# A fused attention and FFN block on one core: first batches brought forward, last contexts by groups, the first maxima's scores made twice

## The reference

```
xn  = (x - mean) / sqrt(var + 1e-5)                      # over the channels
q, k, v = xn @ w.T * s + b                               # 128x128 each, 16 heads of 8 channels
ctx = softmax(q k.T / sqrt(8)) v                         # by head, 256 x 256 scores
att = ctx @ w_o.T * s_o + b_o
h   = s0 * [xn, -xn] @ (+1 or -1 by k0)                  # 256 -> 512
h   = s1 * (2 relu(h)) @ (+1 or -1 by k1)                # 512 -> 512
ffn = s2 * (2 relu(h)) @ (+1 or -1 by k2)                # 512 -> 128
out = x + att + ffn
```

## Time and profile before

| | us |
|---|---|
| median of three runs (lowest, highest) | 313.89 (313.88, 314.91) |
| profiled execution | 313.65 |
| its span | 311.8 |
| PE busy in the span | 280.5 (90%) |
| DVE, ACT, POOL busy | 245.7, 224.8, 131.9 |
| mean granted clock of TensorE | 0.981 |

### The profile page before, as it was taken

One profiled execution on the slowest core, in us unless ns is written; L12 is line 12 of the kernel. 1 busy time (PEld: TensorE's weight loads), 2 busy tenths in 40 slices (PEclk: granted clock), 3 DMA queues, 4 the chain that ended last, 5 costly groups with the idle time before them and its releaser, 6 DMA issues.

```text
span 311.8 us, 8673 instructions
## 1 busy us (share of the span) xinstructions
PE 280.5 (90%) x3220; PEld 179.1 (57%) x3220; DVE 245.7 (79%) x367; ACT 224.8 (72%) x373; POOL 131.9 (42%) x315
## 2 busy tenths in 40 slices
PE   5387879999999999999999999999999877799993
PEld 5255546666666666656666666666666443355651
DVE  4714975889898989898998989898989787688632
ACT  2425356888788787878797888887887867477880
POOL 5233543526363636354454536273636343111201
PEclk9999977999999999999999999999999999799999
DMA  4231323213231414232322223241314141400000
GB/s 122 68 95 38 90 74 90 78 56 102 70 107 52 129 54 125 58 106 61 99 85 88 96 71 112 58 125 48 111 49 127 38 129 36 128 21 4 21 16 20
DMA packets 27387, 23.84 MB, mean 76 GB/s; under 512 B 4674, under 2 KB 24146, under 8 KB 27346
## 3 DMA queue, kind: packets, MB, share of 16 engines
q1 hardware_dynamic: 27218, 22.89, 24.7%
q10 hardware_dynamic: 128, 0.39, 0.4%
HBM read 15.47 MB, written 7.34 MB: 73 GB/s over the span
## 4 chain that ended last, share of the span: by engine, by line
PE 73%; DVE 17%; issue 3%; ACT 3%; POOL 1%; DMA 1%; ACTq 0%; POOLq 0%; DVEq 0%
PE work L947 19%; DVE neg_max L687 14%; PE max_pair L915 14%; PE work L1002 12%; PE exp_pair L935 6%; PE work L970 5%; PE work L1017 5%; PE work L989 4%; PE work L1026 3%; PE work L976 2%; PE work L963 1%; DVE r_lo L713 1%; ACT probs L522 1%; ACT r_hi L576 1%; DMA xin<-x 1%
## 5 line engine op out<-in xcount | busy, mean ns | idle before, releaser
L687 DVE TENSOR_REDUCE neg_max<-max_pair 128x4 f32<-128x1024 f32 x124 | 151.1, 1219 | 34.7 <-PE max_pair L915 32.1
L522 ACT ACTIVATE probs<-exp_pair 128x1024 f32<-128x1024 f32 x124 | 126.5, 1020 | 33.0 <-PE exp_pair L935 31.5
L947 PE MATMUL work<-probs,v_ext 128*32 128x256 f32 x1024 | 62.9, 387 | 0.7 <-ACT ffn L609 0.7
L1002 PE MATMUL work<-r_hi,w 128*128 128x256 f16 x256 | 62.2, 282 | 1.1 <-DVE r_lo L713 1.1
L1002 PE MATMUL work<-r_lo,w 128*128 128x256 f16 x256 | 61.9, 280 | 0.0
L915 PE MATMUL max_pair<-k_rows,q_rows 48*128 48x256 f16 x496 | 49.0, 276 | 11.3 <-DVE neg_max L687 8.5
L713 DVE SCALAR_TENSOR_TENSOR r_lo<-work,r_hi 128x512 f16<-128x512 f32 x64 | 43.3, 677 | 15.9 <-ACT r_hi L576 15.9
L935 PE MATMUL exp_pair<-q_rows,k_rows 51*128 51x256 bf16 x496 | 48.2, 272 | 0.5 <-ACT probs L522 0.5
L576 ACT ACTIVATE r_hi<-work 128x512 f16<-128x512 f32 x64 | 37.8, 591 | 11.4 <-PE work L1002 7.3
L947 PEld LDWEIGHTS work<-probs,v_ext 128*32 128x32 f32 x1024 | 30.5, 111 | 24.6 <-issue 7.7
L915 PEld LDWEIGHTS max_pair<-k_rows,q_rows 48*128 48x128 bf16 x496 | 14.2, 94 | 44.2 <-DVE neg_max L687 23.0
(11 more groups left out here) (102 smaller groups left out, 385.6 us busy)
## 6 DMA issues: line engine op xcount, KB each, us to landing
q_rows<-q_scratch SPq DMA_DIRECT2D x64, 96.0 KB
k_rows<-k_scratch SPq DMA_DIRECT2D x60, 96.0 KB
q_scratch<-q_part SPq DMA_DIRECT2D x16, 192.0 KB, 2.0
xin<-x SPq DMA_DIRECT2D x16, 128.0 KB, 2.2
k_scratch<-k_part SPq DMA_DIRECT2D x16, 128.0 KB, 1.8
out<-outs SPq DMA_DIRECT2D x16, 128.0 KB, 1.8
q_rows<-max_rows SPq DMA_DIRECT2D x64, 6.0 KB
k_rows<-k_scratch ACTq DMA_DIRECT2D x4, 96.0 KB
```

The lines of the kernel that those rows point to most:

```text
L522: nc.scalar.activation(probs[p // GROUP][:, first:first + 2, :, :].rearrange("p h k q -> p (h k q)"), exp_banks(b, p)[:, :], ACT.Exp, scal ...
L687: nc.vector.tensor_reduce(out=neg_max[:, p // GROUP, :, p % GROUP, :], in_=max_banks(b, p)[:, :].rearrange("p (x q k) -> p x q k", x=2, q=TT),
L947: last = mm(bank[VC * j:VC * (j + 1), g * SEQ:(g + 1) * SEQ], v_ext[b % 2][:, kt, HALF * half + head, :], probs[half][:, head, kt, :], sta ...
L1002: last = mm(bank[:, (m % 2) * SEQ:(m % 2 + 1) * SEQ], w1[:, kk, m * P:(m + 1) * P], part[:, kk, :], start=kk == n == 0, stop=kk == FB - 1 ...
```

## The change

The tables are retimed. Batches 1 to 3 get their input work much earlier, from four buffers instead of two or three. The FFN of batches 0 and 1 comes one slot earlier, that of batches 14 and 15 eight slots later than its place instead of sixteen. At the start the attention weights are loaded from ACT's queue, x of four batches early, the FFN weights with a semaphore each. v_ext is zeroed and k_rows filled with ones by DVE (the first k_rows before the statistics of batch 0, the others in slots -4 and 2), instead of POOL's memsets and the DMAs of ones. DVE scales batch 0's q, POOL forms its xT_lo, SP issues its k rows. The scores for the maxima of batches 0 and 1 are computed twice into the same banks. The last batch's second context half is done by its two groups, and DVE alone normalises the last batch's contexts.

```diff
-PE_AT = {"maxT0": 5, "maxT1": 9, ..., "ctx1": 16, "ctx0": 12, "v": 1, ..., "xT": -13, "l0b": -9}
-ACT_AT = {"q_mid": -7, ..., "max0": 5, "v": 1, ..., "max1": 8, ...}
-POOL_AT = {"q_lo": -6, "k_lo": -8, "split0": 4, "split1": 7, "q_rest": -7, "xT_lo": -11, "norm": -18,
-           "xres": -12, "ctxn": 19, "y": 3}
-SP_AT = {"rows": -3, "max0": 7, "k_store": -5, "q_store": -4, "x": -24, "out": 24, "max1": 11}
+PE_AT = {"maxT1": 9, "o": 22, "maxT0": 5, ..., "ctx1": 16, "v": 2, "ctx0": 12, ..., "ctx2": 16}
+ACT_AT = {"q_mid": -7, "v": 2, ..., "max0": 4, "max1": 9, ...}
+POOL_AT = {"k_lo": -8, "norm": -17, "split1": 7, "xres": -10, "q_rest": -7, "q_lo": -7, "xT_lo": -11,
+           "split0": 3, "y": 3, "ctxn": 20}
+SP_AT = {"out": 24, "max1": 11, "max0": 7, "rows": -2, "q_store": -4, "x": -23, "k_store": -6}
...
-FFN_LATER = {0: -7, 1: -1, BATCH - 2: 16, BATCH - 1: 16}
-INPUT_WORK = ("norm", "xT", "xT_lo")
-INPUT_LATER = {1: -22}
+FFN_LATER = {0: -8, 1: -2, BATCH - 2: 8, BATCH - 1: 8}
+INPUT_WORK = ("stats", "meanvar", "norm", "xT", "xT_lo", "xres")
+INPUT_LATER = {0: -18, 1: -23, 2: -14, 3: -12}
+LAST_WORK = ("ctx2", "turned2")
+WARM = {}
+MAX_TIMES = {0: 2, 1: 2}
+K_ONES = (-4, 2)
...
             load_x(0)
-            load_weights()
             load_x(1)
+            sp.dma_start(k0_sb[:, :, :].bitcast(u32), k0.rearrange("(a p) f -> p a f", p=P)).then_inc(k0_loaded, 16)
+            sp.dma_start(k1_sb[:, :, :].bitcast(u32), k1.rearrange("(a p) f -> p a f", p=P)).then_inc(k1_loaded, 16)
+            load_x(2)
...
+            load_x(3)
             store_k(sp, 0)
             store_q(sp, 0)
+            load_k(sp, 0)
             load_q(sp, 0)
-            sp.wait_ge(ones_ready, 3)
-            for n in range(3):
-                for par in range(2):
-                    sp.dma_start(k_rows[n][par * TILE + ROWS:par * TILE + MROWS, :],
...
             variance_root(0, 0)
             variance_root(0, 1)
-            for n in range(2):
-                nc.gpsimd.memset(v_ext[n][:, :, :, :], 0.0).then_inc(v_zeroed, 1)
+            normalise(1)
+            split_xT(nc.gpsimd, pool, 0)
...
+            act.dma_start(w_sb[:, :, :], w4).then_inc(attn_weights_loaded, 16)
+            act.dma_start(sc_sb[:, :], sc7.to_broadcast([P, 7])).then_inc(attn_weights_loaded, 16)
+            act.dma_start(bqkv_sb[:, :], bqkv).then_inc(attn_weights_loaded, 16)
...
+            def turn_last_group(g):
+                dve.wait_ge(ctx_psum, 2 * BATCH + g - 2)
...
+                nc.vector.transpose(turned[:, g, :, :].rearrange("p b c -> p (b c)"), bank[:, 0:SEQ]
+                                    ).then_inc(ctx_turned, 1)
+            def normalise_last(first, n):
...
+                nc.vector.reciprocal(rden[:, groups, :], turned[:, groups, :, DH]).then_inc(tail_step, 1)
+                dve.wait_ge(tail_step, 1 if first == 0 else 2)
+                at_least(dve, ctxT_ready, BATCH - 1)
+                last = nc.vector.tensor_tensor(
...
             nc.vector.memset(max_part[:, :, :], 0.0).then_inc(max_part_zeroed, 1)
+            for n in range(2):
+                nc.vector.memset(v_ext[n][:, :, :, :], 0.0).then_inc(v_zeroed, 1)
+            nc.vector.memset(k_rows[0][:, :], 1.0).then_inc(k_ones_ready, 1)
             token_stats(0)
             mean_and_variance(0)
...
+            token_stats(1)
+            mean_and_variance(1)
+            first_scales()
+            first_layer_weights()
+            scale_first_q()
             split_k(nc.vector, dve, 0)
...
             for s in range(FIRST_SLOT, END_SLOT):
                 for b, p in pair_in(s):
                     maxima(b, p)
+                if s in K_ONES:
+                    nc.vector.memset(k_rows[K_ONES.index(s) + 1][:, :], 1.0).then_inc(k_ones_ready, 1)
...
                 bank = max_banks(b, p)
-                for qt in range(TT):
+                for _, qt in itertools.product(range(MAX_TIMES.get(b, 1)), range(TT)):
...
+            def last_context(g, name):
+                b = BATCH - 1
+                pe.wait_ge(probs_ready, PAIRS * b + 2 * (g + 1))
+                bank = take_bank(name, b)
+                for kt, j in itertools.product(range(TT), range(GROUP)):
...
-            keep_warm(16)
+            keep_warm(11)
```

More of the change, by code:

```diff
@@ L74, in slot_of, with stands @@
     return PAIRS * b + table[work] + later.get(b, 0)
+def stands(work, b):
+    return b == BATCH - 1 or work not in LAST_WORK
 def due(table, s):
-    return [(work, b) for work in table for b in range(BATCH) if slot_of(table, work, b) == s]
+    return [(work, b) for work in table for b in range(BATCH) if stands(work, b) and slot_of(table, work, b) == s]
 def pair_in(s):
@@ L164, in build @@
         ffn = [sb(f"ffn{n}", [P, TT, HID], f32) for n in range(2)]
-        y = [sb(f"y{n}", [P, TT, HID], f32) for n in range(3)]
-        ones = sb("ones", [QPARTS, SEQ], f16)
+        y = [sb(f"y{n}", [P, TT, HID], f32) for n in range(6)]
         probs = [sb(f"probs{n}", [P, HALF, TT, SEQ], f32) for n in range(2)]
@@ L191, in build @@
         bo_loaded = sem("bo_loaded")
-        ffn_weights_loaded = sem("ffn_weights_loaded")
-        x_loaded = [sem(f"x_loaded{n}") for n in range(2)]
+        k0_loaded = sem("k0_loaded")
+        k1_loaded = sem("k1_loaded")
+        k2_loaded = sem("k2_loaded")
+        x_loaded = [sem(f"x_loaded{n}") for n in range(4)]
         k_stored = [sem(f"k_stored{n}") for n in range(2)]
@@ L880, in place @@
                 return (early and EARLY.index(work) - 1000 or slot_of(PE_AT, work, b), list(PE_AT).index(work))
-            FILLS = [sorted((place(work, b), work, b) for work in BANK if BANK[work] == n for b in range(BATCH))
+            FILLS = [sorted((place(work, b), work, b) for work in BANK if BANK[work] == n for b in range(BATCH) if stands(work, b))
                      for n in range(4)]
@@ L939, in context @@
             def context(b, half):
+                if b == BATCH - 1 and half == 1:
+                    last_context(2, "ctx1")
+                    return
                 pe.wait_ge(probs_ready, PAIRS * b + PAIRS // 2 * (half + 1))
@@ L950, in context @@
                 last.then_inc(ctx_psum, 1)
+            def last_context(g, name):
[3 more added lines that the diff above has]
+                for kt, j in itertools.product(range(TT), range(GROUP)):
+                    head = GROUP * g + j
+                    last = mm(bank[VC * j:VC * (j + 1), 0:SEQ], v_ext[b % 2][:, kt, head, :],
+                              probs[1][:, head % HALF, kt, :], start=kt == 0, stop=kt == TT - 1)
+                last.then_inc(ctx_psum, 1)
             def maxima_to_rows(b, half):
@@ L962, in turn_x @@
                 for t in range(TT):
-                    last = nc.tensor.transpose(bank[:, t * P:(t + 1) * P], xn[:, t, :], ident[:, :])
+                    last = nc.tensor.transpose(bank[:, t * P:(t + 1) * P], xn[b % 2][:, t, :], ident[:, :])
                 last.then_inc(xT_psum, 1)
@@ L969, in project @@
                 bank = take_bank(work, b)
-                mm(bank[:, 0:SEQ], w_sb[:, n, :], xT[b % 2][:, :], start=True, stop=True).then_inc(ready, 1)
+                mm(bank[:, 0:SEQ], w_sb[:, n, :], xT[b % 4][:, :], start=True, stop=True).then_inc(ready, 1)
             def project_v(b):
@@ L988, in layer0 @@
                     for n, part in enumerate((xT_hi, xT_lo)):
-                        last = mm(bank[:, m * SEQ:(m + 1) * SEQ], w0[:, c:c + P], part[b % 3][:, :],
+                        last = mm(bank[:, m * SEQ:(m + 1) * SEQ], w0[:, c:c + P], part[b % 4][:, :],
                                   start=n == 0, stop=n == 1)
```

214 lines of the change are left out of this document (112 added, 102 removed).

## The result

The changed kernel is slower, by some 0.9%: median 316.56 us of 20 executions (313.57 to 321.21) against 313.21 of 20 of the kernel before (310.02 to 314.91); ratio 1.0088, 95% interval 1.0058 to 1.0117. The prediction was 306.2. Executions of one kernel differ by up to 8.6 us (e4), and TensorE's mean granted clock differs between them too (0.955 to 0.981 in the changed kernel); a ratio leaves out those more than 1.5% above their kernel's fastest, a median here does not.

The account below looks back on a forecast made before the run. TensorE's work was taken to set 60 to 240 us; time lay in the start, the stretch without FFN work and the end. Gains of 4.2+0+0+0.6+0.4+2.2 = 7.4 us gave 306.2, range 304.0 to 311.0.

Parts of the forecast that it names:

- the price of a fill: VectorE's fills at the start and in slots -4 and 2: 0.38 us per v_ext, 0.62 per k_rows.
- A clock of 0.7 between 35 and 50: Listed sign of being wrong: granted clock (1.00 is 2.4 GHz) at 0.7 between 35 and 50 us.
- the steady bound of 1.6: Slots 16 to 104: sum 0 a batch, from -0.15 to +0.15, so 1.6 us either way.
- Setup, -3.1: Start to slot 0: fills end under the wait for x, second layer at 14.9, slot 0 at 26.4, 3.1 us earlier.
- The first rival: Slow fills, 0.9 ns an element: 1.8 us at the start, 0.75 at slot -4, 1.3 at slot 2; 310.1 us, chance 0.24.
- Slots 0 to 8, -1.0: 14.94 us less 1.7 for a slow stretch plus 0.62 for a fill gives 13.9.
- Slots 8 to 16, 0: Second pass of scores adds 1.7 us, holding the clock saves some 1.6; 17.6 us, nothing gained.
- Steady batches, 0 from -1.6 to 1.6: Slots 16 to 104: v in slot 2 gains 0.1 a batch, ACT's early copy holds the next scores by 0.1; sum 0.
- The rival on the other side: Slower than before: ACT's early copy passes its wait to TensorE every batch, losing 11.8 us; 318.0 us, chance 0.06.
- Slots 104 to 128, -0.6: With FFN eight slots late, 15.8 us for slots 104 to 112, then twice 15.7; sum 47.2, 0.6 less.
- To the last context, -0.4: From slot 128: ACT copies 0.7 later, then four exponentials with a context between; 12.25 us, 0.4 less.
- The end, -2.2: From the last context: eight matmuls instead of 32 save 1.4 us, one turn 0.3, reciprocal and product on VectorE 0.5.

Follow-up runs that it names:

- e4: The changed kernel with ScalarE's copies of the maxima back in slots 5 and 8 instead of 4 and 9; 314.06 us.
- e14: The changed kernel with the three k_rows fills written as 1024 words of 32 bits instead of 2048 of 16, same bytes; 311.92 us.
- e1: The changed kernel with all fills undone: POOL zeroes v_ext again, DMAs bring the rows of ones; 311.51 us.
- e6: e5 with the scores for the maxima of batches 0 and 1 made once instead of twice; 310.38 us.
- e13: The changed kernel with the second and third k_rows fills moved from VectorE's slots -4 and 2 to POOL, before the loop; 311.78 us.
- e2: The changed kernel with the scores for the maxima of batches 0 and 1 made once; 312.66 us.
- e3: The changed kernel with the FFN of batches 14 and 15 sixteen slots late again instead of eight; 317.47 us.
- e9: e5 with the three attention weight loads issued by SP again, between x of batch 0 and x of batch 1; 309.62 us.
- e10: e5 with eleven unused transpositions on TensorE in the gap before the first batch's second first-layer group; 308.90 us.
- e15: e5 with the changes of e9 and e10 together, plus exponentials' scores made three times in four slots of the stretch without FFN work; 308.81 us.
- e5: The changed kernel with fills undone as in e1, v back in slot 1 and ScalarE's maxima copies back in slots 5 and 8; 310.19 us.
- e8: The kernel before with one part alone: scores for the maxima of batches 0 and 1 made twice; 315.58 us.

## Why the prediction was wrong

The profile is 10.7 us longer than the forecast. Of these, 3.4 arose in slots 0 to 8, 2.8 in slots 104 to 128, 1.5 in the setup, 1.5 in the steady batches, 1.2 ahead of the last context and 0.5 at the end; slots 8 to 16 gave 0.3 back. Two steps failed above all: the price of a fill, and the clock, which was forecast to hold from 25 us on and fell in three places. A clock of 0.7 between 35 and 50 was named as a sign of being wrong, and it came. The range's lower end doesn't follow from its sentence: 306.2 less the steady bound of 1.6 is 304.6, not 304.0.

**Setup, -3.1; measured -1.6.** The price of a fill failed: "0.38 us for each v_ext (1024) and 0.62 for a k_rows (2048)". They took 0.91 and 1.76, 0.86 to 0.89 ns an element. I took the slope from a single short row and passed over POOL's 0.9 ns beside it. The page that spoke against me, the Trainium skill (VectorE: DVE Perf Modes, "Zero memsets can be issued as uint32 (trn2)"), is borne out in that, for e14 shows that elements are paid and not bytes. The three fills took 3.6 us, less than the 4.3 estimated from it. Yet at the start this cost little (e1: 0.24 us), because "it is free from 1.00 to 3.03, when x has landed" had failed too: with the loads side by side the statistics began at 4.25 and 4.46 and the weights were used at 5.7 and 6.1 (e6, e1), before at 3.03 and 4.77, and that covered the fills. The statistics began 2.1 us later than forecast (5.20, not 3.1), xn was ready 2.0 later (8.23, not 6.2) and the second layer started 1.6 later (16.49, not 14.9). From there to slot 0 it took 11.44, as forecast, though the terms given for that stretch (10.33, twice 0.3, 0.87) add up to 11.8 and not to 11.5. The first rival, "1.8 us after x", had the right price in the wrong place at the start, and "holds r_lo of batch 1 by 0.75" is what e1 showed (0.86, of which 0.14 came from the start). The second layer's half pace was in the kernel before too, and I didn't see it.

**Slots 0 to 8, -1.0; measured +2.4.** The step that cost most. "A fill of 0.62" in a list of VectorE's busy times was 1.76, put between two reduces for which TensorE waits; it stopped TensorE for 2.43 us, and behind the stop the clock fell. e1, e13 and e14 show that these fills cost: without them, or with each at 0.91, slots 0 to 8 take 13.00, 13.00 and 15.18 instead of 17.34, and the kernel 3.1 to 3.9 us less by the ratios. That the stop makes the clock fall is likely, not shown: it fell between 35 and 45 in all five profiles with a fill of 0.91 or 1.76 in slot 2 (the changed kernel, e2, e3, e4, e14), but also in three of nine with the second pass and no fill there (e9, e10, e15). The rival priced such a fill at 1.3 and left the clock out.

**Slots 8 to 16, 0; measured -0.3.** Right in size: the clock held, and the second pass took 1.3 (e2) of the 1.7 it was given. The reason, that the second pass holds the clock, fits all profiles but two: with it the clock held from 45 on in twelve of thirteen, without it only in e2. It costs what a fall there costs (17.0 to 17.2 against 17.1 to 17.6 by the reduces), so nothing is gained, as forecast.

**Steady batches, 0 from -1.6 to 1.6; measured +1.5.** Inside the bounds at the bad end. "Gain 0.1" by v failed: slot 1, whose next scores then wait for the reduce, gave back 0.26 a batch, and slot 2 took 0.29 more (0.40 with the copies put back). The rival on the other side, 11.8 us from ScalarE's copies, did not happen.

**Slots 104 to 128, -0.6; measured +2.2.** "Twice 15.7" held nearly (16.16 and 15.58). "15.8" for 104 to 112 was 18.28, because the clock fell there. e1, e2, e4, e13 and e14 have 15.57 to 15.67 in that place, so the forecast was right for an execution without the fall. What decides whether it falls there is open.

**To the last context, -0.4; measured +0.75.** "ACT now copies after an exponential, 0.7 later" was right (the store is issued 4.92 us after the last reduce, before 4.21); what it does was not: the wait for the store became 2.38 us, and the clock fell behind it. With the copies put back and the clock up it takes 11.5 (e4, e5), less than the 12.25 forecast.

**The end, -2.2; measured -1.7.** Right in mechanism; the term that was too large is "eight matmuls instead of 32 save 1.4". The trace counts 16 behind the last exponential, and from their start to the turn it takes 1.14 us instead of 2.00: 0.86 saved. The turn saved 0.27 and the reciprocal and product with their hops 0.53, as forecast.

One fault runs through these: I read the falls of one execution as places of the kernel, each to be removed. They differ from execution to execution: e10 has e5's program but for eleven transpositions before 15 us, and in the stretch without FFN work its clock held where e5's fell, and over the 35 executions of the kernel before that stand beside e5 to e8 the mean granted clock lies between 0.949 and 0.992. By span x 2 x (1 - clock), an estimate, an average execution of the kernel before spent 16 to 19 us at the lower level (it depends on the set of executions), of the changed kernel 19.5, of e13 12. The change was to remove falls, and its executions spend no less time at the lower level.

## What to carry to other kernels

Ahead of putting an instruction into a loop paced by two engines that wait for each other, ask what the other engine does during its whole length, restart included; work that is due any time belongs on an engine that idles, once you have seen what it slows beside it (e13), in the widest elements it can have (e14). A job moved out of a full slot frees only what the slot's other engine leaves free. Clock falls of one profiled execution are a sample: judge a change that aims at them by many executions and by the mean granted clock.
